# Attention projections as three fp32r products of high and low parts, and an earlier transpose of x

## The chip, the cores and the metric

The kernel is one program on one NeuronCore of a Trainium2 chip. Its engines run side by side, each with its own instruction queue: TensorE (PE; its weight loads are listed as PEld), VectorE (DVE), ScalarE (ACT), GpSimd (POOL) and SyncE (SP). They wait for each other through semaphores. The metric is the device time of one launch in microseconds, lower is better.

## The reference, cut to what matters

Three blocks follow each other on 8192 tokens of width 256, in fp32: an expert block, a linear attention, and the expert block again.

```python
x = x + 0.5 * _L0_ffn_ref(_layernorm(x), Wr, W1, W3, W2)   # 8 experts, top 2, capacity 2560
x = x + _L0_attn_ref(_layernorm(x), Wq, Wk, Wv, Wc, Ltri)
x = x + 0.5 * _L0_ffn_ref(_layernorm(x), Wr, W1, W3, W2)

def _L0_attn_ref(X, Wq, Wk, Wv, Wc, Ltri):                 # 4 sequences of 2048, 16 heads of 16
    Q, K, V = ((X @ W.T).reshape(B, L, H, d) for W in (Wq, Wk, Wv))
    KVc = cumsum(einsum('blhd,blhe->blhde', K, V), axis=1) # causal, no softmax
    Y = einsum('blhd,blhde->blhe', Q, KVc)
    Bm = tril(Ltri) @ swapaxes(tril(Ltri))
    Y = einsum('hed,blhd->blhe', Bm, Y).reshape(B, L, D)
    return Y @ Wc.T
```

## The kernel before

Four phases run one after the other. `route_phase` normalizes x, takes the router's logits and writes a table of tokens by expert; it also centres the attention's weights (`Setup`). `expert_phase` runs twice. Between its two runs, `middle_phase` does the attention, the second norm and the second routing. The expert phases already multiply through `mm3` (lines 79 to 83): each fp32 operand is kept as a high part rounded to fp32r and a low part, the rest, and a product is high x high + high x low + low x high, three fp32r matmuls.

The change is in `middle_phase`. It treats 64 chunks of 128 tokens, in 8 groups of 8. The order is written out by hand: the loop over `STEPS` is unrolled, and step n does on every engine, in program order, work of several chunks. c is the chunk's place in its group. On PE a step is: the products for q and k of chunk n+2 (`project_qk`, 8 fp32 matmuls of 128x128 weights on 128 columns), from c = 3 on the ranks of the router, v and the logits of n+2 (`project_v`, 2 matmuls of 264 columns), the scores of n+1 (`scores`, 8 matmuls on 32-row tiles), the state's product of n (`attend_state`) and the masked scores by v (`attend`, 16 matmuls on 32-column tiles), the state's update (`update`), two transposes of k (`turn_k`), two transposes of x of n+3 (`turn_x`), and the output product of n (`project_out`). One fp32 matmul shows in the trace as two records of PE and two of PEld.

ACT copies results out of PSUM: k, v, logits, q three times, then y (`keep_y`), k's rows (`keep_krow`) and the transposed x (`keep_x`), which `project_qk` of the next step waits for. DVE masks the scores of n+1 (`mask`, four operations), masks the state (`keep_state`), adds the attention's output to x (`add_out`, which the next `attend` waits for, `x2_ready`) and takes statistics. In the steps with c = 0, 1, 3 and 4, from the second group on, DVE also does the group's norms and routing, and at the end of `place_rest` (c = 3) POOL starts 16 indirect DMAs which write the table, 128 rows of 8 bytes each. `turn_x` writes into the PSUM bank `xv`, which also holds v, the logits and the ranks; so it waits until v was kept (`v_kept`) and, for c = 3, until the ranks were read (`rank_read`).

Of the kernel before, what the change touches and what calls it, by code (L numbers as in the profile page):

```python
# [382 lines left out]
class Setup:  # L383


    def __init__(self, m, k, inputs, bank_b, bank_m):
        self.k, self.inputs, self.pb, self.pm = k, inputs, bank_b, bank_m
        self.raw_qk = m.sb("su_raw_qk", [P, KD, 2 * D])
        self.raw_vr = m.sb("su_raw_vr", [P, KD, WV])
        self.wc_ext = m.sb("su_wc_ext", [P, KD, WV])  # L390
        self.wcn = m.sb("su_wcn", [P, KD, D])
        self.lt = m.sb("su_lt", [P, KD, HD])
        self.low = m.sb("su_low", [P, P])
        self.mean = m.sb("su_mean", [P, P])
# [5 lines left out]
        self.tri_ready = m.sem("su_tri_ready")  # L400
        self.bbd_made, self.bbd_ready = m.sem("su_bbd_made"), m.sem("su_bbd_ready")
        self.wcr_made, self.wcr_ready = m.sem("su_wcr_made"), m.sem("su_wcr_ready")
        self.fold_made = m.sem("su_fold_made")
# [84 lines left out]
        ins.then_inc(self.means_made, 1)  # L488

    def center(self, dve):  # L490

        k = self.k
        dve.wait_ge(self.means_made, 1)
        for kk in range(KD):
            dve.tensor_tensor(k.wqk[:, kk, :], self.raw_qk[:, kk, :], self.pm[:, 0:2 * D], ALU.subtract)
            ins = dve.tensor_tensor(k.wvr[:, kk, :], self.raw_vr[:, kk, :], self.pb[:, 0:WV], ALU.subtract)
        ins.then_inc(self.centered, 1)

    def heads(self, pe):

        pe.wait_ge(self.tri_ready, KD)
        pe.wait_ge(self.centered, 1)
        for a in range(KD):
            ins = pe.matmul(self.pb[:, a * P:(a + 1) * P], self.lbd[:, a, :], self.lbd[:, a, :], start=True, stop=True)
        ins.then_inc(self.bbd_made, 1)
        for a in range(KD):
            for kk in range(KD):
                ins = pe.matmul(self.pm[:, a * E:(a + 1) * E], self.wcn[:, kk, a * P:(a + 1) * P],
                                self.k.wvr[:, kk, D:WV], start=(kk == 0), stop=(kk == KD - 1))
        ins.then_inc(self.wcr_made, 1)  # L510

    def keep_heads(self, act):
# [52 lines left out]
def route_phase(nc, k, attention, x_in, xn_out, x1_out, out, tables, w, slot_a, raw, raw_loaded, tiles_out):  # L565
# [4 lines left out]
    with ExitStack() as ctx:  # L570
# [30 lines left out]
        with nc.Block() as block:  # L601
# [25 lines left out]
            def _(act):  # L627
# [8 lines left out]
                def step(g, s, i):  # L636
                    act.wait_ge(x_loaded[s], 16 * i + 16)
                    act.dma_start(group(x1_g, g), xin[s][:]).then_inc(x_copied[s], 16)
                    r.keep_xnT(act, g)
                    act.dma_start(group(xn_g, g), xn[s][:]).then_inc(xn_stored[s], 16)  # L640
                    r.weigh(act, g)
                    if isinstance(g, int) and g == 1:
                        su.keep_heads(act)

                rounds(act, step)
                su.keep_fold(act)
# [8 lines left out]
            def _(dve):  # L655
# [5 lines left out]
                def step(g, s, i, last=False):  # L661
                    r.choose(dve, g)
                    r.place(dve, g, s, 16 * NR * TOPK * i)
                    if not last:
                        ln(g + 2, s, i + 1)
                    if isinstance(g, int) and g == 0:
                        su.center(dve)

                su.numbers(dve)
                dve.memset(zeros[:], 0.0)  # L670
# [322 lines left out]
def middle_phase(nc, k, x1_in, xn_out, x2_out, table, tiles_out):  # L993
# [6 lines left out]
    with ExitStack() as ctx:  # L1000
# [4 lines left out]
        xT = [m.sb(f"xT{b}", [P, KD, P]) for b in range(2)]  # L1005
# [18 lines left out]
        n1_ready = m.sem("n1_ready")  # L1024
        n2_ready = m.sem("n2_ready")
        xt_made = m.sem("xt_made")
        xT_ready = m.sem("xT_ready")
        qk_made = m.sem("qk_made")
        k_kept = m.sem("k_kept")
# [29 lines left out]
        with nc.Block() as block:  # L1059
# [28 lines left out]
            def _(pe):  # L1088
# [9 lines left out]
                def project_qk(n):  # L1098
                    pe.wait_ge(xT_ready, n + 1)
                    wait(pe, kr_kept, n)  # L1100
                    for blk in range(2 * KD):
                        for kk in range(KD):
                            ins = pe.matmul(qk[:, blk * P:(blk + 1) * P], k.wqk[:, kk, blk * P:(blk + 1) * P],
                                            xT[n % 2][:, kk, :], start=(kk == 0), stop=(kk == KD - 1))
                    ins.then_inc(qk_made, 1)

                def project_v(n):
                    for kk in range(KD):
                        ins = pe.matmul(xv[:, 0:WV], xT[n % 2][:, kk, :], k.wvr[:, kk, :],
                                        start=(kk == 0), stop=(kk == KD - 1))  # L1110
                    ins.then_inc(v_made, 1)

                def scores(n):
# [57 lines left out]
                for n in STEPS:  # L1171
# [6 lines left out]
                        project_v(n + 2)  # L1178
                    if chunk(n + 1):
                        scores(n + 1)  # L1180
                    if chunk(n):
                        attend(n)
                        update(n)
                    if chunk(n + 2):
                        turn_k(n + 2)
                    if chunk(n + 3):
                        if c == 3 and g >= 1:
                            pe.wait_ge(r.rank_read, g)
                        turn_x(n + 3)
                    if chunk(n):  # L1190
                        project_out(n)
                r.count(pe, MGS)
# [2 lines left out]
            def _(act):  # L1195
                def keep_x(n):
                    act.wait_ge(xt_made, n + 1)
                    act.activation(xT[n % 2][:], xv[:, 0:D].rearrange("p (a t) -> p a t", a=KD),
                                   ACT.Copy).then_inc(xT_ready, 1)

                def keep_k(n):
                    act.wait_ge(qk_made, n + 1)
# [38 lines left out]
                for n in STEPS:  # L1241
# [3 lines left out]
                    if chunk(n + 2):  # L1245
                        keep_k(n + 2)
                        keep_v(n + 2)
                        keep_q(n + 2)
                    if chunk(n):
# [3 lines left out]
                    if chunk(n + 3):  # L1253
                        keep_x(n + 3)
# [5 lines left out]
            def _(dve):  # L1260
# [8 lines left out]
                def keep_state(n):  # L1269
                    if n % CB == CB - 1:  # L1270
# [35 lines left out]
                for c in range(MG):  # L1306
                    stats_x1(0, c)
                moments_x1(0)
                for n in STEPS:
                    g, c = divmod(n, MG)  # L1310
                    if c == 3 and g >= 1:
# [1 line left out]
                        r.place_first(dve, g - 1)  # L1313
                    if chunk(n + 1):
                        mask(n + 1)
                    if chunk(n):
                        keep_state(n)
                    if c == 0 and g >= 1:
# [16 lines left out]
class Constants:  # L1335


    def __init__(self, m):
# [17 lines left out]
        self.wqk = m.sb("wqk", [P, KD, 2 * D])  # L1356
        self.wvr = m.sb("wvr", [P, KD, WV])
        self.fold = m.sb("fold", [P, KD, WV])


# [45 lines left out]
```

## Time and profile before

| what | value |
|---|---|
| time, median of 3 runs | 3372.84 us (3371.47 to 3377.68) |
| the profiled execution's own time | 3342.54 us |
| its span, first to last instruction | 3340.8 us |
| mean granted TensorE clock | 0.940 of full speed |
| PE / PEld busy | 2977.2 / 2868.5 us, 89% / 86% |
| DVE, ACT, POOL busy | 1416.7, 1200.6, 1175.6 us |

Busy times of engines overlap. A PE record's duration is that of one matmul from start to modelled end, and consecutive ones overlap, so the pace of a run of matmuls is read from its starts: (length of the merged row less one record's duration) / (count less one). A granted clock of 1.00 is 2.4 GHz, 0.50 is 1.2 GHz. The profiled execution was 30 us shorter than the median of the timed runs.

### The profile page before, as it was taken

Reading aid. Unit: us, or ns where it says so; the run is one execution under the profiler, and the core shown is the slowest. Engines: PE = TensorE matmul, PEld = TensorE weight load, DVE = VectorE, ACT = ScalarE, POOL = GpSimd, SP = SyncE. Lnnn points to the kernel's source line nnn. Section 1 sums busy time; section 2 is a strip of 40 time slices with the busy share of each in tenths; the row PEclk is TensorE's granted clock in tenths of the full one; section 3 lists DMA queues with packets and bytes.
Section 4 is the critical chain, followed back from the end, with each engine's and each line's share of the span. In section 5 each row is a group of like instructions: output and inputs, shape, how many; then the busy total and the mean of one; then the engine's idle time right before and its main releaser. Section 6 shows DMA issues by size and latency. Waiting matters only on the chain. (4 is left out here: it accounts for less than half of the span.)

```text
span 3340.8 us, 68238 instructions
## 1 busy us (share of the span) xinstructions
PE 2977.2 (89%) x25886; PEld 2868.5 (86%) x25887; DVE 1416.7 (42%) x3386; ACT 1200.6 (36%) x2383; POOL 1175.6 (35%) x1520
## 2 busy tenths in 40 slices
PE   3429999999999999979877888499999999999998
PEld 3319999999999999968766666499999999999998
DVE  5533343443434434326655555334343434434342
ACT  1113343443434434324333333234343434434343
POOL 4563333343333333320222211433333333333333
PEclk7559999999999999989988889699999999999999
DMA  6423131222213121120111101321331322223111
GB/s 206 128 78 68 31 70 28 67 49 49 65 31 69 28 66 31 30 55 27 39 39 39 52 27 33 95 50 28 69 66 28 69 31 64 55 44 66 28 31 28
DMA packets 153036, 180.48 MB, mean 54 GB/s; under 512 B 22064, under 2 KB 126768, under 8 KB 152944
## 3 DMA queue, kind: packets, MB, share of 16 engines
q0 software_dynamic: 61376, 72.67, 13.7%
q1 hardware_dynamic: 73824, 88.72, 8.6%
q10 hardware_dynamic: 17744, 17.89, 1.6%
q8 instruction: 55, 0.90, 0.1%
q14 instruction: 37, 0.30, 0.0%
HBM read 107.84 MB, written 71.37 MB: 54 GB/s over the span
## 5 line engine op out<-in xcount | busy, mean ns | idle before, releaser
L975 DVE TENSOR_TENSOR e_hid<-e_ps,e_gate 128x512 f32<-128x512 f32 x540 | 373.2, 691 | 1048.6 <-ACT e_gate L935 1012.1
L81 PE MATMUL e_ps<-e_xT_hi,c_wa_hi 128*128 128x256 f32 x2144 | 608.0, 284 | 3.9 <-DVE e_xT_lo L969 3.0
L81 PE MATMUL e_ps<-e_xT_hi,e_wb_hi 128*128 128x256 f32 x2176 | 609.5, 280 | 0.0
L82 PE MATMUL e_ps<-e_xT_lo,e_wb_hi 128*128 128x256 f32 x2176 | 609.1, 280 | 0.0
L83 PE MATMUL e_ps<-e_xT_hi,e_wb_lo 128*128 128x256 f32 x2176 | 609.0, 280 | 0.0
L82 PE MATMUL e_ps<-e_xT_lo,c_wa_hi 128*128 128x256 f32 x2144 | 607.5, 283 | 0.0
L83 PE MATMUL e_ps<-e_xT_hi,c_wa_lo 128*128 128x256 f32 x2144 | 603.5, 281 | 0.0
L979 DVE TENSOR_TENSOR e_h_lo<-e_hid,e_h_hi 128x512 fp32r<-128x512 f32 x540 | 374.3, 693 | 376.9 <-ACT e_h_hi L937 295.3
L935 ACT ACTIVATE e_gate<-e_ps 128x512 f32<-128x512 f32 x540 | 322.0, 596 | 545.1 <-PE e_ps L83 519.6
L937 ACT ACTIVATE e_h_hi<-e_hid 128x512 fp32r<-128x512 f32 x540 | 341.3, 632 | 421.6 <-DVE e_hid L975 407.5
L813 POOL DMA_INDIRECT x<-e_yrow,e_y_token x140 | 225.5, 1611 | 655.4 <-ACT e_yrow L948 632.4
L813 POOL DMA_INDIRECT out<-e_yrow,e_y_token x138 | 222.4, 1611 | 652.8 <-ACT e_yrow L948 350.4
L82 PEld LDWEIGHTS e_ps<-e_xT_lo,e_wb_hi 128*128 128x128 f32 x2176 | 409.4, 188 | 0.0
L83 PEld LDWEIGHTS e_ps<-e_xT_hi,e_wb_lo 128*128 128x128 f32 x2176 | 409.3, 188 | 0.0
L81 PEld LDWEIGHTS e_ps<-e_xT_hi,e_wb_hi 128*128 128x128 f32 x2176 | 409.3, 188 | 0.0
L81 PEld LDWEIGHTS e_ps<-e_xT_hi,c_wa_hi 128*128 128x128 f32 x2144 | 404.1, 188 | 5.9 <-issue 5.9
L83 PEld LDWEIGHTS e_ps<-e_xT_hi,c_wa_lo 128*128 128x128 f32 x2144 | 408.3, 190 | 0.0
L82 PEld LDWEIGHTS e_ps<-e_xT_lo,c_wa_hi 128*128 128x128 f32 x2144 | 404.2, 189 | 0.0
L805 POOL DMA_INDIRECT e_xrow<-normed_rows,e_token x274 | 332.4, 1213 | 176.9 <-POOL e_token L834 118.7
L81 PE MATMUL e_psy<-e_wb_hi,e_h_hi 128*128 128x256 f32 x1088 | 313.2, 288 | 0.0
L353 POOL DMA_INDIRECT table<-mi_r_entry,mi_r_entry_at x128 | 125.3, 979 | 517.5 <-DVE mi_r_entry_at L347 364.2
L83 PE MATMUL e_psy<-e_wb_hi,e_h_lo 128*128 128x256 f32 x1088 | 307.2, 282 | 0.0
(232 smaller groups left out, 5447.1 us busy)
## 6 DMA issues: line engine op xcount, KB each, us to landing
raw<-w SPq DMA_DIRECT2D x204, 256.0 KB
r_xin<-x SPq DMA_DIRECT2D x8, 1024.0 KB
x<-r_xin ACTq DMA_DIRECT2D x8, 1024.0 KB
normed_rows<-r_xn ACTq DMA_DIRECT2D x8, 1024.0 KB
mi_x<-x SPq DMA_DIRECT2D x8, 1024.0 KB, 8.0
out<-mi_x SPq DMA_DIRECT2D x8, 1024.0 KB, 5.3
normed_rows<-mi_xn SPq DMA_DIRECT2D x8, 1024.0 KB
e_xrow<-normed_rows,e_token POOLq DMA_INDIRECT x274
```

What stands on the lines that cost most here:

```text
L81: pe.matmul(out, a[0], b[0], start=first, stop=False)
L82: pe.matmul(out, a[0], b[1], start=False, stop=False)
L83: return pe.matmul(out, a[1], b[0], start=False, stop=last)
L353: pool.indirect_dma_start(self.table, bass.IndirectOffsetOnAxis(ap=self.entry_at[b][:, c, j:j + 1], axis=0), self.entry[b][:, c, j, :], No ...
L805: pool.indirect_dma_start(xrow[:, sub, :], None, xn, bass.IndirectOffsetOnAxis(ap=token[:, sub:sub + 1], axis=0), bounds_check=ROWS - 1, o ...
L813: pool.indirect_dma_start(acc, bass.IndirectOffsetOnAxis(ap=y_token[:, sub:sub + 1], axis=0), yrow[:, sub, :], None, bounds_check=ROWS - 1 ...
L935: act.activation(gate[:, j % 2, :], ps1[j % 2][:], ACT.Silu).then_inc(gated, 1)
L937: act.activation(h[0][:, j * 512:(j + 1) * 512], hid[:, j % 2, :], ACT.Copy).then_inc(h_high, 1)
L975: dve.tensor_tensor(hid[:, j % 2, :], ps3[j % 2][:], gate[:, j % 2, :], ALU.mult).then_inc(hid_ready, 1)
L979: dve.tensor_tensor(h[1][:, at], hid[:, j % 2, :], h[0][:, at].bitcast(F32), ALU.subtract).then_inc(h_ready, 1)
```

## The change

The weights of q, k, v and logits are kept in high and low parts, split once in `Setup` (two operations on ACT, two on DVE; the heads' product reads the unsplit ones). `xT` has a high part, which ACT's `keep_x` now writes rounded to fp32r, and a low part, which a new DVE operation `low_x` writes (PSUM less high part). The products go through `mm3`. On PE `turn_x` of n+3 stands in front of `attend`, on ACT `keep_x` in front of `keep_y`, on DVE `low_x` between `mask` and `keep_state`.

```diff
     def center(self, dve):
         for kk in range(KD):
-            dve.tensor_tensor(k.wqk[:, kk, :], self.raw_qk[:, kk, :], self.pm[:, 0:2 * D], ALU.subtract)
-            ins = dve.tensor_tensor(k.wvr[:, kk, :], self.raw_vr[:, kk, :], self.pb[:, 0:WV], ALU.subtract)
+            dve.tensor_tensor(self.raw_qk[:, kk, :], self.raw_qk[:, kk, :], self.pm[:, 0:2 * D], ALU.subtract)
+            ins = dve.tensor_tensor(self.raw_vr[:, kk, :], self.raw_vr[:, kk, :], self.pb[:, 0:WV], ALU.subtract)
+    def split_high(self, act):
+        act.wait_ge(self.centered, 1)
+        act.activation(self.k.wqk[0][:], self.raw_qk[:], ACT.Copy)
+        act.activation(self.k.wvr[0][:], self.raw_vr[:], ACT.Copy).then_inc(self.w_split, 1)
+    def split_low(self, dve):
+        dve.wait_ge(self.w_split, 1)
+        dve.tensor_tensor(k.wqk[1][:], self.raw_qk[:], k.wqk[0][:].bitcast(F32), ALU.subtract)
+        dve.tensor_tensor(k.wvr[1][:], self.raw_vr[:], k.wvr[0][:].bitcast(F32), ALU.subtract)
...
                 def project_qk(n):
-                            ins = pe.matmul(qk[:, blk * P:(blk + 1) * P], k.wqk[:, kk, blk * P:(blk + 1) * P],
-                                            xT[n % 2][:, kk, :], start=(kk == 0), stop=(kk == KD - 1))
+                            ins = mm3(pe, qk[:, blk * P:(blk + 1) * P],
+                                      [w[:, kk, blk * P:(blk + 1) * P] for w in k.wqk],
+                                      [t[:, kk, :] for t in xT[n % 2]], kk == 0, kk == KD - 1)
                 def project_v(n):
-                        ins = pe.matmul(xv[:, 0:WV], xT[n % 2][:, kk, :], k.wvr[:, kk, :],
-                                        start=(kk == 0), stop=(kk == KD - 1))
+                        ins = mm3(pe, xv[:, 0:WV], [t[:, kk, :] for t in xT[n % 2]], [w[:, kk, :] for w in k.wvr],
+                                  kk == 0, kk == KD - 1)
...
                     if chunk(n + 1):
                         scores(n + 1)
+                    if chunk(n + 3):
+                        if c == 3 and g >= 1:
+                            pe.wait_ge(r.rank_read, g)
+                        turn_x(n + 3)
                     if chunk(n):
                         attend(n)
                         update(n)
                     if chunk(n + 2):
                         turn_k(n + 2)
-                    if chunk(n + 3):
-                        if c == 3 and g >= 1:
-                            pe.wait_ge(r.rank_read, g)
-                        turn_x(n + 3)
...
+                def low_x(n):
+                    dve.wait_ge(xT_high, n + 1)
+                    dve.tensor_tensor(xT[n % 2][1][:], xv[:, 0:D].rearrange("p (a t) -> p a t", a=KD),
+                                      xT[n % 2][0][:].bitcast(F32), ALU.subtract).then_inc(xT_ready, 1)
...
                     if chunk(n + 1):
                         mask(n + 1)
+                    if chunk(n + 3):
+                        low_x(n + 3)
                     if chunk(n):
                         keep_state(n)
```

One ordinary step on PE, before: `mi_qk` and `mi_xv` are the PSUM banks of q/k and of v/x, `c_wqk` and `c_wvr` the weights, `mi_sc` the scores, `mi_yo` the attention's output, `mi_kv` the state.

```order
755 L1103 MATMUL mi_qk<-mi_xT0,c_wqk 128x128 x8
756 L1109 MATMUL mi_xv<-c_wvr,mi_xT0 128x264 x2
757 L1119 MATMUL mi_sc<-mi_qeo1,mi_kT1 128x256 x8
758 L1127 MATMUL mi_yo<-mi_qT1,mi_state0 128x128 x2
759 L1139 MATMUL mi_yo<-mi_prob0,mi_vpad1 32x128 x16
760 L1153 MATMUL mi_kv<-mi_vpad1,mi_krow0 128x128 x2
761 L1160 MATMUL mi_qk<-c_ident,mi_kT0 128x128 x2
762 L1094 MATMUL mi_xv<-c_ident,mi_x1 128x128 x2
763 L1166 MATMUL mi_yo<-c_fold,mi_yT0 128x264 x2
```

The same step of the changed kernel, from the last of its 24 matmuls for q and k:

```order
946 L83 MATMUL mi_qk<-mi_xT_hi0,c_wqk_lo 128x128
947 L81 MATMUL mi_xv<-c_wvr_hi,mi_xT_hi0 128x264
948 L82 MATMUL mi_xv<-c_wvr_lo,mi_xT_hi0 128x264
949 L83 MATMUL mi_xv<-c_wvr_hi,mi_xT_lo0 128x264
950 L81 MATMUL mi_xv<-c_wvr_hi,mi_xT_hi0 128x264
951 L82 MATMUL mi_xv<-c_wvr_lo,mi_xT_hi0 128x264
952 L83 MATMUL mi_xv<-c_wvr_hi,mi_xT_lo0 128x264
953 L1134 MATMUL mi_sc<-mi_qeo1,mi_kT1 128x256 x8
954 L1108 MATMUL mi_xv<-c_ident,mi_x1 128x128 x2
955 L1142 MATMUL mi_yo<-mi_qT1,mi_state0 128x128 x2
956 L1154 MATMUL mi_yo<-mi_prob0,mi_vpad1 32x128 x16
```

The transposes of x moved from behind those of k to behind the scores, and the two projections are 24 and 6 matmuls instead of 8 and 2.

On DVE, a step with c = 1 of the changed kernel (`mi_prob` is the masked scores, `mi_state` the masked state, `mi_r_lg` the router's logits):

```order
508 L1307 SCALAR_TENSOR_TENSOR mi_x2<-mi_yo,mi_n11_rstd,mi_x1 128x256
509 L133 BN_STATS mi_n21_stats<-mi_x2 128x6
509 L133 BN_STATS mi_n10_stats<-mi_x1 128x6 x2
510 L1280 TENSOR_TENSOR mi_prob0<-mi_sc,c_causal 128x512 x4
511 L1295 TENSOR_TENSOR mi_xT_lo0<-mi_xv,mi_xT_hi0 128x256
512 L1289 TENSOR_TENSOR mi_state0<-mi_kv,c_same_head 128x256
513 L264 TENSOR_TENSOR mi_r_lg<-mi_lgs,mi_n20_rstd 128x64
```

Line 511 is new; all the rest stands as before, one place later.

## Rows read from the trace of the kernel before

**Rows 1.** The attention phase as one window, columns as in rows 2.
```profile
1483.00:2097.00 614.00, 507.58 (x5415) 415.04 (x5415) 350.12 (x1282) 224.29 (x649) 109.61 (x112) 0.90 0.12 39
```

**Rows 2.** Windows of steps 23, 25 to 29: us, PE, PEld, DVE, ACT, POOL, clock.
```profile
1703.98:1711.35 7.37, 7.37 (x85) 6.16 (x84) 3.86 (x8) 2.97 (x9) 0.00 (x0) 1.00 0.00 0
...
1718.73:1726.59 7.86, 7.44 (x85) 6.16 (x84) 6.49 (x26) 3.22 (x10) 0.00 (x0) 1.00 0.15 50
1726.59:1734.34 7.75, 7.45 (x86) 6.16 (x85) 7.27 (x41) 4.15 (x13) 0.00 (x0) 1.00 0.00 0
1734.34:1742.02 7.68, 7.68 (x94) 6.46 (x93) 5.53 (x17) 3.93 (x12) 0.00 (x0) 1.00 0.01 2
1742.02:1763.08 21.06, 9.23 (x85) 6.67 (x83) 6.03 (x22) 3.74 (x12) 14.20 (x15) 0.77 0.02 2
1763.08:1772.38 9.30, 9.30 (x85) 8.08 (x85) 3.71 (x23) 3.89 (x11) 1.46 (x2) 0.79 0.35 116
```

**Rows 3.** Timeline of step 23: start us, us, engine, line, instruction, idle before it.
```profile
1703.98 1.95 PE L1103 MATMUL mi_qk<-mi_xT,c_wqk 128*128 128x128 f32 x16
1705.76 1.06 PE L1109 MATMUL mi_xv<-c_wvr,mi_xT 128*128 128x264 f32 x4
1706.75 1.15 PE L1119 MATMUL mi_sc<-mi_qeo,mi_kT 32*128 32x256 f32 x16
...
1707.22 0.17 ACT L1220 ACTIVATE mi_lgx<-mi_xv 128x8 f32<-128x8 f32 x1
...
1707.82 0.71 PE L1127 MATMUL mi_yo<-mi_qT,mi_state 128*128 128x128 f32 x4
1707.96 2.48 DVE L1265 TENSOR_TENSOR mi_prob<-mi_sc,c_causal 128x512 f32<-128x512 f32 x4 [2.70 <-PE mi_sc L1119]
...
1710.36 0.42 DVE L1274 TENSOR_TENSOR mi_state<-mi_kv,c_same_head 128x256 f32<-128x256 f32 x1
```

**Rows 4.** Pace of matmuls: timeline, instructions by line, one window in the experts.
```profile
35.43 3.64 PE L249 MATMUL r_lg<-c_wr,r_r_xnT 128*128 128x8 f32 x32
...
L249 PEld LDWEIGHTS r_lg<-c_wr,r_r_xnT x256: 186/333/338, 17.2 to 197.2; 128*128 128x128 f32 x128
...
L81 PEld LDWEIGHTS e_ps<-e_xT_hi,e_wb_hi x2176: 186/188/194, 419.4 to 3322.1; 128*128 128x128 f32 x198
...
L302 PEld LDWEIGHTS mi_xv<-mi_r_chosen,c_ones x56: 95/96/131, 1583.3 to 2093.9; 128*128 128x128 bf16 x56
...
1300.00:1310.00 10.00, 10.00 (x86) 1.00 0.06 2
```

**Rows 5.** Timeline of DVE in steps 24 to 27.
```profile
1718.24 0.64 DVE L138 BATCH_NORM_AGGREGATE mi_n_mv<-mi_n_stats 128x2 f32<-128x6 f32 x8
...
1724.04 2.47 DVE L1265 TENSOR_TENSOR mi_prob<-mi_sc,c_causal 128x512 f32<-128x512 f32 x4
1726.42 0.41 DVE L1274 TENSOR_TENSOR mi_state<-mi_kv,c_same_head 128x256 f32<-128x256 f32 x1
...
1731.78 2.47 DVE L1265 TENSOR_TENSOR mi_prob<-mi_sc,c_causal 128x512 f32<-128x512 f32 x4
...
1738.10 0.22 DVE L315 TENSOR_TENSOR mi_r_pos<-mi_xv,c_region 128x64 f32<-128x64 f32 x1 [1.83 <-ACT mi_lgx L1220]
...
1739.63 2.48 DVE L1265 TENSOR_TENSOR mi_prob<-mi_sc,c_causal 128x512 f32<-128x512 f32 x4
```

**Rows 6.** Timeline of step 28, from POOL's first indirect DMA.
```profile
1744.62 0.98 POOL L353 DMA_INDIRECT table<-mi_r_entry,mi_r_entry_at  x1 [58.05 <-DVE mi_r_entry_at L347]
...
1758.13 0.38 ACT L1224 ACTIVATE mi_yT<-mi_yo 128x256 f32<-128x256 f32 x1 [11.69 <-remote]
...
1763.08 3.78 PE L1103 MATMUL mi_qk<-mi_xT,c_wqk 128*128 128x128 f32 x16 [2.39 <-ACT mi_xT L1198]
...
1767.32 0.23 DVE L1285 SCALAR_TENSOR_TENSOR mi_lgs<-mi_yo,mi_n_rstd,mi_lgx 128x8 f32<-128x8 f32 x1 [6.63 <-remote]
```

**Rows 7.** Timeline of the route phase, DVE behind POOL's second batch.
```profile
83.94 0.22 DVE L257 TENSOR_SCALAR r_r_lg<-r_lg 128x64 f32<-128x64 f32 x1 [13.79 <-remote]
```

More of the change, by code:

```diff
@@ L400, in __init__ @@
         self.tri_ready = m.sem("su_tri_ready")
+        self.w_split = m.sem("su_w_split")
         self.bbd_made, self.bbd_ready = m.sem("su_bbd_made"), m.sem("su_bbd_ready")
@@ L490, in center @@
     def center(self, dve):
-        k = self.k
         dve.wait_ge(self.means_made, 1)
         for kk in range(KD):
-            dve.tensor_tensor(k.wqk[:, kk, :], self.raw_qk[:, kk, :], self.pm[:, 0:2 * D], ALU.subtract)
-            ins = dve.tensor_tensor(k.wvr[:, kk, :], self.raw_vr[:, kk, :], self.pb[:, 0:WV], ALU.subtract)
+            dve.tensor_tensor(self.raw_qk[:, kk, :], self.raw_qk[:, kk, :], self.pm[:, 0:2 * D], ALU.subtract)
+            ins = dve.tensor_tensor(self.raw_vr[:, kk, :], self.raw_vr[:, kk, :], self.pb[:, 0:WV], ALU.subtract)
         ins.then_inc(self.centered, 1)
+    def split_high(self, act):
[3 more added lines that the diff above has]
+    def split_low(self, dve):
+        k = self.k
+        dve.wait_ge(self.w_split, 1)
+        dve.tensor_tensor(k.wqk[1][:], self.raw_qk[:], k.wqk[0][:].bitcast(F32), ALU.subtract)
+        dve.tensor_tensor(k.wvr[1][:], self.raw_vr[:], k.wvr[0][:].bitcast(F32), ALU.subtract)
     def heads(self, pe):
@@ L508, in heads @@
                 ins = pe.matmul(self.pm[:, a * E:(a + 1) * E], self.wcn[:, kk, a * P:(a + 1) * P],
-                                self.k.wvr[:, kk, D:WV], start=(kk == 0), stop=(kk == KD - 1))
+                                self.raw_vr[:, kk, D:WV], start=(kk == 0), stop=(kk == KD - 1))
         ins.then_inc(self.wcr_made, 1)
@@ L643, in step @@
                         su.keep_heads(act)
+                        su.split_high(act)
                 rounds(act, step)
@@ L667, in step @@
                         su.center(dve)
+                    if isinstance(g, int) and g == 1:
+                        su.split_low(dve)
                 su.numbers(dve)
@@ L1004, in middle_phase @@
         xn2 = m.sb("xn2", [P, 2, MG, D])
-        xT = [m.sb(f"xT{b}", [P, KD, P]) for b in range(2)]
+        xT = [[m.sb(f"xT_{part}{b}", [P, KD, P], F32R) for part in ("hi", "lo")] for b in range(2)]
         qT = [m.sb(f"qT{b}", [P, KD, P]) for b in range(3)]
@@ L1026, in middle_phase @@
         xt_made = m.sem("xt_made")
+        xT_high = m.sem("xT_high")
         xT_ready = m.sem("xT_ready")
@@ L1197, in keep_x @@
                     act.wait_ge(xt_made, n + 1)
-                    act.activation(xT[n % 2][:], xv[:, 0:D].rearrange("p (a t) -> p a t", a=KD),
-                                   ACT.Copy).then_inc(xT_ready, 1)
+                    act.activation(xT[n % 2][0][:], xv[:, 0:D].rearrange("p (a t) -> p a t", a=KD),
+                                   ACT.Copy).then_inc(xT_high, 1)
                 def keep_k(n):
@@ L1248, in _ @@
                         keep_q(n + 2)
+                    if chunk(n + 3):
+                        keep_x(n + 3)
                     if chunk(n):
@@ L1252, in _ @@
                         keep_krow(n + 2)
-                    if chunk(n + 3):
-                        keep_x(n + 3)
                     if 1 <= c <= 4 and g >= 1:
@@ L1308, in _ @@
                 moments_x1(0)
+                low_x(0)
                 for n in STEPS:
@@ L1315, in _ @@
                         mask(n + 1)
+                    if chunk(n + 3):
+                        low_x(n + 3)
                     if chunk(n):
@@ L1355, in __init__ @@
         self.wr = m.sb("wr", [P, KD, E])
-        self.wqk = m.sb("wqk", [P, KD, 2 * D])
-        self.wvr = m.sb("wvr", [P, KD, WV])
+        self.wqk = [m.sb("wqk_hi", [P, KD, 2 * D], F32R), m.sb("wqk_lo", [P, KD, 2 * D], F32R)]
+        self.wvr = [m.sb("wvr_hi", [P, KD, WV], F32R), m.sb("wvr_lo", [P, KD, WV], F32R)]
         self.fold = m.sb("fold", [P, KD, WV])
```

## The prediction, made before the changed kernel ran

> **What bounds the kernel now.** I read the split by phases first, then the attention phase step by step, then one step's timeline. (Each of rows 1 and 2 gives busy time in the order PE, PEld, DVE, ACT, POOL.) The changed projections run only between 1483 and 2097 us, 614 us in all, in which PE is busy 507.6, DVE 350.1 and ACT 224.3 us [rows 1]. The reader is to see in the windows that an ordinary step takes 7.37 us and PE has work in all of it, while DVE has 3.86 and ACT 2.97 us [rows 2]: there PE is the bound, and what the change adds to PE goes into the time one for one. The steps with c = 1, 2 and 3 are different: they take 7.86, 7.75 and 7.68 us, and DVE is busy 6.49, 7.27 and 5.53 of them [rows 2]; DVE is nearly as much the bound as PE. The step with c = 4 takes 21.06 us, of which PE has work in 9.23. It is no ordinary wait: from 3 us after POOL's first indirect DMA, ACT waits 11.69 us for the result of `attend`, and the groups behind it come through one by one, the output product's only at 1767.3 [rows 6]. PE's results come at a crawl as long as POOL issues its 16 table writes.
>
> **The q and k projection.** It removes 16 passes (8 fp32 matmuls, two records each) and adds 24 fp32r matmuls of 128 columns. The 16 took 1705.76 - 1703.98 = 1.78 us, 0.111 each [rows 3]. No row shows an fp32r matmul of 128 columns, so its pace is bounded. From above by the same type on twice the columns: 86 matmuls, nearly all fp32r of 256 columns, in 10 us, 0.116 each [rows 4]. From below by the stream alone: 256 fp32r columns in 0.116 makes 0.058 for 128. What decides is the weight load. L249 streams 8 columns only, and its 32 passes still come (3.64 - 0.18)/31 = 0.112 us apart at full clock (the 0.18 is one record) [rows 4]. So a 128x128 fp32 weight load alone holds the array 0.11 us, whatever streams behind it. Is an fp32r load the same? Its shortest record is 186 ns, as L249's, against 95 for a bf16 load [rows 4]: same load, same floor. I take 0.116, between ends 0.112 and 0.125 (some slack for the change of operand order) if the floor holds. 24 x 0.116 = 2.78, less 1.78: +1.00 us a step.
>
> The Trainium skill, "TensorE: Matmul & The Clock Gate", section "Back-to-back issue gap", gives about 81 ns as the sustained pace of a weight load and a matmul at 128 columns. By it the 24 would take 1.94 us, +0.16. The trace does not bear that out for fp32: 112 ns with 8 columns. I keep it as a rival. The same page, Part 3, says that weight loads overlap matmuls in flight only if the row group differs. By that load and stream would add up; but 256 columns at 0.116 with a load that alone needs 0.112 leave no room for a sum, so the trace speaks against that one, too.
>
> **The v and logits projection.** Four passes of 264 columns and the change to 32-row tiles took 1706.75 - 1705.76 = 0.99 us [rows 3], about 0.225 a pass and 0.09. Now six fp32r matmuls of 264 columns, 0.116 to 0.12 each: 0.79. That is -0.19. Sum of both: **+0.81 us** per ordinary step, 8.18 instead of 7.37 (with 0.112: +0.7; with 0.125: +1.0).
>
> **The moved transposes.** They cost PE the same two records in either place. At their new place they wait for ACT to have kept v and the logits, which was done at 1707.39, 0.43 us before the product behind the scores began [rows 3], so nothing. ACT writes the high part as soon as q is kept, before y is ready. The output product follows two transposes sooner behind `attend` than before; that can cost at most these two records, 0.2 us, if y should come late. In the step shown PE waits for nobody, so I take 0.
>
> **The low part on DVE.** One subtraction 128x256 from PSUM; nearest row the state's mask, 0.41 to 0.42 us [rows 3]. In an ordinary step it stands behind the mask of the scores: scores now start at 3.57 in the step, the mask 1.21 later at 4.8 (1707.96 less 1706.75) [rows 3], 2.4 us, low part ready at 7.7. The next projection is due at 8.18: hidden with 0.5 us to spare. That cover is gone in the tight steps, all times from the start of the step's q and k products:
> - c = 0: 8.18 (+0.81). DVE's norms start behind the state, at 8.1.
> - c = 1: from the norm's start to the next mask DVE needs 1724.04 - 1718.24 = 5.8 us [rows 5], so this mask starts at 8.1 + 5.8 - 8.18 = 5.7, and 2.4 and 0.41 later the low part is ready: 8.55 instead of 7.86, +0.7.
> - c = 2: from the state's start to the next mask 1731.78 - 1726.42 = 5.36 [rows 5]; mask at 5.36, low part at 8.2: 8.2 instead of 7.75, +0.45. The waits of `attend` for `add_out`, which lengthened these two steps, are gone: PE comes there 1 us later.
> - c = 3: the mask stands behind `place_first`, which waits for the kept logits at 3.76 and starts the mask at 5.29 (1738.10 and 1739.63 [rows 5], less 1734.34 [rows 2]). Both shift by the 0.81 of PE; mask 6.1, low part at 8.95: 8.95 instead of 7.68, +1.27. PE waits here for DVE some 0.75 us.
> Sum of the four: +3.2 us.
>
> **c = 4 and 5.** PE gets its +0.81 twice. The crawl has the length of POOL's batch, about 20 us, from wherever it starts; I take what it costs as unchanged. What PE does behind it runs at half clock: 16 passes in 3.78 us [rows 6], 0.21 apart, twice the 0.111. 24 of them are +1.7 us instead of +1.0, and v gains 0.38 instead of 0.19: +0.5 more. Sum +2.1. Of the four results that come late one by one before the next projection can start, the x transposes are no longer one; at up to 2 us each that could give back 0 to 2 us a group. I take 0 since PE works the same list off during the crawl.
>
> **c = 6 and 7:** 2 x 0.81 = +1.6.
>
> **Sum.** A group with routing: 3.2 + 2.1 + 1.6 = 6.9, seven of them 48.5. The first group has none: 8 x 0.81 = 6.5. The two projections at the start at half clock: +1. In the route phase the split of the weights puts some 2.5 us on ACT and 2.5 on DVE (1552 columns per partition each at the 0.41 us per 256), where DVE then idles 13.79 us behind POOL's batch [rows 7]: hidden, 0.5 for the rest. The experts are untouched. Total **+57 us**. On the profiled execution's 3342.5 us (span 3340.8 and 1.7 around it) that makes 3399.5. The timed runs lie 30 us above the profiled one; I put the difference on their median: 3372.8 + 57 = **3430 us**, +1.7%.
>
> **The rivals.**
> - A, fp32r at 128 columns runs no faster than the fp32 product it stands for, two passes or 0.223 each (256 columns is the only width the trace shows). Then +3.57 - 0.19 = +3.4 a step, 64 steps: +216, 3590. For it: no row at 128. Against it: the pace per column is the type's, and 264 of v isn't concerned. 6%.
> - B, load and stream do not overlap: 0.112 + 0.053 = 0.165, +1.98 a step, about +127, 3500. 4%.
> - C, faster: an fp32r load is quick as bf16's (95 ns records against 186) and the stream decides, 0.058. Then -0.39 - 0.19 = -0.58 a step where PE binds. It decides from 0.082 down: there PE's sum is zero. DVE's new 0.41 then binds c = 1 to 3 and costs +1 there; a group 1 - 5 x 0.58 = -1.9, the whole -13 - 5 = -18: 3355. Against it the length of the load records. 6%.
> - D, 0.081 to 0.085 as in the skill's pace: PE's sum is zero, and DVE's low part costs about 1 us a group: +7, 3380, at the edge of no change. 4%.
> - E, within my forecast: the crawl gets shorter by 2 us a group (-14), or longer, because more of `attend` falls into it (+14).
>
> **How the numbers follow.** About 0.2% (7 us) is what a measurement can tell from no change. Forecast with E: 80%. Its own range: 0.112 takes 0.1 off the steps where PE binds, 6 in all, and with the shorter crawl 51 - 14 = +37; 0.125 adds 0.22 to each of 64, and with the longer crawl 71 + 14 = +85. The outer ends need two things at once; I give 3405 to 3458, which leaves out A to D. Faster: C, 6%. Same: half of D and a little, 3%. Slower: 91%.
>
> **What would show it.** In the changed profile the 24 matmuls of L81 to L83 into `mi_qk` start 0.112 to 0.118 us apart at full clock, with load records of about 188 ns; ordinary steps take 8.1 to 8.3 us with PE busy throughout; in c = 3 PE waits for DVE's low part; the windows outside 1483 to 2150 stay as they are. It is wrong if the pace is below 0.09 or above 0.13, if ordinary steps show PE waiting for `xT_lo`, or if the step with c = 4 changes by more than 3 us.

## The result, and the profile after

| what | before | after |
|---|---|---|
| time, median of 4 runs each, on one chip | 3372.15 us (3365.35 to 3377.68) | 3460.09 us (3456.95 to 3460.75) |
| ratio after / before | | 1.026, 95% interval 1.024 to 1.028 |
| profiled execution, span | 3340.8 us | 3458.8 us |
| mean granted TensorE clock | 0.940 | 0.926 |

The changed kernel is 88 us slower. The forecast was slower by 57, 3430 us in a range up to 3458: the direction was right, 31 us were missing.

The same steps as in [rows 2], as windows of the changed kernel: the attention phase, then steps 23 to 29 (us, then PE, PEld, DVE, ACT, POOL busy, clock, DMA).

```profile
1478.90:2170.00 691.10, 559.21 (x5851) 478.59 (x5851) 355.35 (x1258) 216.44 (x626) 104.46 (x109) 0.86 0.11 34
1759.62:1767.69 8.07, 8.07 (x97) 7.12 (x95) 4.20 (x9) 2.98 (x9) 0.00 (x0) 1.00 0.00 0
1767.69:1775.75 8.06, 8.06 (x96) 7.11 (x95) 4.19 (x9) 2.98 (x9) 0.00 (x0) 1.00 0.78 239
1775.75:1784.10 8.35, 8.35 (x96) 7.09 (x94) 7.28 (x32) 3.40 (x11) 0.00 (x0) 1.00 0.08 26
1784.10:1792.18 8.08, 8.08 (x95) 7.05 (x95) 7.60 (x42) 3.94 (x13) 0.00 (x0) 1.00 0.01 2
1792.18:1801.15 8.97, 8.61 (x105) 7.32 (x103) 6.09 (x19) 4.58 (x13) 0.00 (x0) 1.00 0.00 0
1801.15:1827.95 26.80, 9.97 (x94) 8.23 (x95) 6.31 (x22) 4.04 (x12) 15.65 (x16) 0.73 0.02 2
1827.95:1840.42 12.47, 12.47 (x97) 10.89 (x95) 7.03 (x30) 3.24 (x10) 0.00 (x0) 0.62 0.25 85
```

The reader is to see that an ordinary step is full of PE and 0.70 us longer than before (8.07 against 7.37), that the steps with c = 1, 2 and 3 take 8.35, 8.08 and 8.97 us (forecast 8.55, 8.2 and 8.95), and that the surprise stands in the last two rows: c = 4 and 5 grew from 21.06 + 9.30 = 30.36 to 39.27 us, by 8.9, where 2.1 was forecast. Not all of the 8.9 is the change: the two profiles are of executions 118 us apart (spans 3340.8 and 3458.8), while the timed medians are 88 apart, and a second profile of the kernel before has longer steps here than the first (below).

One ordinary step in the timeline, against [rows 3]:

```profile
1759.84 0.28 PE L82 MATMUL mi_qk<-mi_xT_lo,c_wqk_hi 128*128 128x128 f32 x1
1762.30 0.27 PE L83 MATMUL mi_qk<-mi_xT_hi,c_wqk_lo 128*128 128x128 f32 x1
1762.41 0.34 PE L81 MATMUL mi_xv<-c_wvr_hi,mi_xT_hi 128*128 128x264 f32 x1
1763.29 1.15 PE L1134 MATMUL mi_sc<-mi_qeo,mi_kT 32*128 32x256 f32 x16
1764.37 0.44 PE L1108 MATMUL mi_xv<-c_ident,mi_x 128*128 128x128 f32 x2
1764.84 0.38 ACT L1213 ACTIVATE mi_xT_hi<-mi_xv 128x256 fp32r<-128x256 f32 x1
1766.90 0.41 DVE L1295 TENSOR_TENSOR mi_xT_lo<-mi_xv,mi_xT_hi 128x256 fp32r<-128x256 f32 x1
1767.69 0.39 PE L81 MATMUL mi_qk<-mi_xT_hi,c_wqk_hi 128*128 128x128 f32 x1
```

From the step's start (1759.62) to the first matmul for v (1762.41) the 24 matmuls take 2.79 us, 0.116 each; that includes a longer gap behind the first. From the second (1759.84) to the last (1762.30) they come 0.112 apart. v with the change to the scores takes 1763.29 - 1762.41 = 0.88. Both together are 3.67 us, where before they were 2.77 (1.78 + 0.99); the rest of the step gave 0.2 back. The low part is ready at 1767.31, 7.69 in the step and 0.38 before PE wants it.

The step with c = 4, against [rows 6]:

```profile
1803.87 0.98 POOL L353 DMA_INDIRECT table<-mi_r_entry,mi_r_entry_at  x1 [69.53 <-DVE mi_r_entry_at L347]
1806.66 1.19 PE L1154 MATMUL mi_yo<-mi_prob,mi_vpad 128*32 128x128 f32 x30
1807.42 0.38 ACT L1213 ACTIVATE mi_xT_hi<-mi_xv 128x256 fp32r<-128x256 f32 x1 [1.00 <-PE mi_xv L1108]
1823.11 0.98 POOL L353 DMA_INDIRECT table<-mi_r_entry,mi_r_entry_at  x1 [0.30 <-issue]
1825.96 0.38 ACT L1239 ACTIVATE mi_yT<-mi_yo 128x256 f32<-128x256 f32 x1 [18.16 <-remote]
1826.71 0.42 DVE L1289 TENSOR_TENSOR mi_state<-mi_kv,c_same_head 128x256 f32<-128x256 f32 x1 [17.20 <-remote]
```

PE now reaches `attend` later behind the start of the batch: it begins 1806.66 - 1803.87 = 2.79 us behind POOL's first write (2.65 to 3.06 over the groups), where it began at most 1.9 behind it before. ACT then waits 18.16 us for y, not 11.69, and gets it 22.1 us behind the first write (18.7 to 22.9 over the groups), 13.5 before (10.7 to 13.5). And the start of the phase, which had no row in the forecast:

```profile
1492.33 2.71 DVE L133 BATCH_NORM_STATS2 mi_n_stats<-mi_x 128x6 f32<-128x256 f32 x8 [5.11 <-DMA mi_x<-x]
1493.14 0.38 ACT L1213 ACTIVATE mi_xT_hi<-mi_xv 128x256 fp32r<-128x256 f32 x1 [17.66 <-PE mi_xv L1108]
1498.86 0.42 DVE L1295 TENSOR_TENSOR mi_xT_lo<-mi_xv,mi_xT_hi 128x256 fp32r<-128x256 f32 x1
1499.33 0.47 PE L81 MATMUL mi_qk<-mi_xT_hi,c_wqk_hi 128*128 128x128 f32 x1 [6.29 <-DVE mi_xT_lo L1295]
```

The first projection now waits 6.29 us for a low part that stands behind all of DVE's statistics of the first group; before, it needed only ACT's copy, which was there after 0.53 us:

```profile
1483.29 3.78 PE L1103 MATMUL mi_qk<-mi_xT,c_wqk 128*128 128x128 f32 x16 [0.53 <-ACT mi_xT L1198]
```

The clock follows: from the first transposes of x to the first scores the changed kernel takes 23.4 us, all of them at a granted clock of 0.50, the kernel before 15.3 us at 0.61, and 1.00 from there on, where the changed kernel still has 0.50 up to 1528.

### The profile page after: what moved, and what is told of

Same layout as the page of the kernel before. It is cut to its first block and busy times, and to the rows that moved or that the text cites. A ratio compares the mean times of both kernels' runs of the same rounds, so it can differ in the third digit from the quotient of the medians.

```text
span 3458.8 us, 69586 instructions
## 1 busy us (share of the span) xinstructions
PE 3037.9 (88%) x26526; PEld 2939.3 (85%) x26527; DVE 1441.7 (42%) x3452; ACT 1204.6 (35%) x2385; POOL 1175.9 (34%) x1520
## 3 DMA queue, kind: packets, MB, share of 16 engines
q0 software_dynamic: 61376, 72.67, 12.8%
```

## The experiments

Theory 1 was that the price in ordinary steps is as forecast, and that what is missing is PE's results behind POOL's batch: PE takes some 0.6 us per pass there, whatever the size of the pass, and the change leaves more passes of `attend` inside. Against it stood rivals, above all that the moved transposes cost the time, and that where the batch falls in the step does not matter. The expectations number them. They count the step with c = 4 from its scores to the next step's scores (20.8 to 25.5 us in the first profile, 29.3 to 30.7 in the changed kernel's), and so do the lengths of these steps given below; the windows above count from its q and k products. Each group of runs was on one chip with the kernel before beside it; differences between kernels are compared within a group, or as ratios.

**The first chip: before 3372.52 us (3366.15 to 3381.91, 7 runs).**

*e1, the transposes back at their old place, the low part behind the state.* The edit on PE; ACT's copy and DVE's low part move in the same way.

```diff
-                    if chunk(n + 3):
...
-                        turn_x(n + 3)
                     if chunk(n):
                         attend(n)
                         update(n)
                     if chunk(n + 2):
                         turn_k(n + 2)
+                    if chunk(n + 3):
...
+                        turn_x(n + 3)
```

> The changed kernel with the transposes of x, ACT's high part and DVE's low part (now behind the state's mask) back at their old places; only the arithmetic is changed. Theory 1 (during POOL's 16 table writes PE gets through one matmul pass in some 0.65 us, whatever its size, and the 32 passes of attend now fall into that stretch because POOL's first write comes 3.06 us before attend, not 1.89): here POOL starts still about 3.1 us before attend, so the step with c = 4 stays at 29 to 31 us and the time within 10 us of 3460. Rival 2 (the moved transposes push attend into the slow stretch): attend comes 0.22 us earlier, y is released 2 to 4 us earlier in each of seven groups: 3430 to 3445.

Measured: 3480.48 us (3478.46 to 3481.13), ratio 1.0314 (1.0289 to 1.0339), against 1.026 of the changed kernel. The ordinary step is 8.48 us, 0.41 over the changed kernel's:

```profile
1772.65 0.38 PE L1108 MATMUL mi_xv<-c_ident,mi_x 128*128 128x128 f32 x2
1773.54 0.42 DVE L1295 TENSOR_TENSOR mi_xT_lo<-mi_xv,mi_xT_hi 128x256 fp32r<-128x256 f32 x1 [0.36 <-ACT mi_xT_hi L1213]
1774.02 0.33 PE L81 MATMUL mi_qk<-mi_xT_hi,c_wqk_hi 128*128 128x128 f32 x1
```

The low part ends at 1773.96 and PE starts right behind it. So the move costs nothing; it keeps a chain of transpose, ACT, DVE off the step's end, and `attend` is as late behind the batch without it (2.8 to 3.2 us), with steps c = 4 of 29.6 to 30.4 us, as expected. The rival that the move costs time falls. That the time would stay within 10 us of 3460, as theory 1 had it, missed: it is 20 away, since the part of the low part was not in it.

*e3, the first low part ahead of the statistics.*

```diff
                 r.start(dve)
+                low_x(0)
                 for c in range(MG):
                     stats_x1(0, c)
                 moments_x1(0)
-                low_x(0)
```

> The changed kernel with DVE's very first low part put in front of the first group's statistics. In the trace of the changed kernel the first projection waits 6.3 us for it. Theory: the attention phase starts 5 to 6 us earlier, time 3454. Rival (the half-clock stretch at the start sets it, the wait is hidden in it): no change, 3460.

Measured: 3450.36 us (3449.45 to 3458.02), ratio 1.0233 (1.0205 to 1.026); from the first transposes of x to the first scores 18.09 us instead of 23.38. The wait at the start is real and avoidable, worth 5 us in the profile; by the time alone it is not clear of the changed kernel, whose ratio (1.024 to 1.028) touches this one:

```profile
1492.23 0.42 DVE L1295 TENSOR_TENSOR mi_xT_lo<-mi_xv,mi_xT_hi 128x256 fp32r<-128x256 f32 x1 [6.32 <-ACT mi_xT_hi L1213]
1492.58 2.70 DVE L133 BATCH_NORM_STATS2 mi_n_stats<-mi_x 128x6 f32<-128x256 f32 x8
```

*e4 and e5, the kernels before and after without the attention phase's 128 indirect writes* (the second expert phase then works on unfilled entries).

```diff
-                for g in range(MGS):
-                    r.enter(pool, g, g % 2)
...
```

> The kernel before without the 128 indirect DMAs of the attention phase that write the second routing table (the second expert phase then works on unfilled entries, with the same counts). Theory 1: the long steps with c = 4 (21 to 25 us) become ordinary ones of 7.4 to 8, and the half-clock stretches go: seven groups lose 15 to 17 us each, 3372 - 112 = 3260. Rival (these steps wait for something else, as code loading or the router's chain): within 10 us of 3372.

> The changed kernel without the same 128 indirect DMAs. Theory 1: no step over 9 us; seven groups lose some 22 us each, 3460 - 154 = 3306; and against the kernel before without writes it is +50 to +65 us (0.69 us a step, the tight steps, the start) instead of +88. Rival 3 (the extra of the step with c = 4 comes from the low part's hand-over, ACT to DVE to PE): the difference between the two kernels without writes stays 80 to 90 us.

Measured: 3213.51 us (3211.41 to 3214.97), ratio 0.9523, and 3272.04 us (3265.51 to 3274.03), ratio 0.9692. Their distance is **58.5 us**, against 88 with the writes: the change without the writes costs what was forecast (50 to 65 were expected), and some 29 us come with them. Both times are below theory 1's, which had 3260 and 3306, in part because the last batch, which the second experts wait for, is gone too: from the last output product to their first matmul e4 takes 27.4 us, the kernel before 51.1. In the kernel before without writes the step with c = 4 is an ordinary one:

```profile
1725.41:1732.79 7.38, 7.38 (x85) 6.16 (x85) 5.40 (x20) 3.95 (x11) 0.00 (x0) 1.00 0.15 53
```

**The second chip: before 3340.15 us (3333.47 to 3344.42, 7 runs).** The first run here is the kernel before again.

> The kernel before, profiled once more. Its first profile lies 30 us under its timed runs. If that profile was a quick execution, this one shows a time near 3370 us, a route phase some 10 us longer (the first expert matmul at 267 to 272 us instead of 258, as in every other profile so far), and in the attention phase results of attend released later than 13.5 us behind POOL's first write. If profiling itself makes it quicker, it shows 3342 again.

Its profiled execution took 3349.39 us, with steps c = 4 of 21.1 to 26.6 us and y 11.4 to 13.6 us behind the first write. Neither expectation is decided, since this chip's own timed runs are at 3340; but a profiled execution is not quicker than timed ones here. So the profile that the forecast rested on was most likely taken on a quicker chip than its timed runs; the chip of the first profile is not on record.

*e6, the changed kernel, each batch held back until the scores of the step with c = 4; e7 and e8, after and before with two writes behind the scores of each of eight steps.*

```diff
                 for g in range(MGS):
+                    wait_alone(pool, sc_made, min(8 * g + 14, NCH), k.passed)
                     r.enter(pool, g, g % 2)
```

```diff
                 for g in range(MGS):
-                    r.enter(pool, g, g % 2)
+                    wait_alone(pool, r.entry_ready, g + 1, k.passed)
+                    for c in range(MG):
+                        if c % 1 == 0:
+                            wait_alone(pool, sc_made, min(8 * g + 14 + c // 1, NCH), k.passed)
+                        for j in range(TOPK):
+                            pool.indirect_dma_start(
...
```

> The changed kernel, but POOL starts each batch of 16 table writes only when the scores of the c = 4 step are made, some 3.4 us later. Theory 1 (a pass costs about 0.65 us in the slow stretch, whatever its size): the stretch now falls on the next step's projections, 30 long passes worth 3.4 us of ordinary time, instead of attend's 32 short ones worth 1.0; steps c = 4 and 5 together 34.5 instead of 39.2 us, time 3428. Rival 4 (the stretch costs its own length wherever it falls): 3460.

> The changed kernel with each group's 16 table writes spread over eight steps, two behind each step's scores. If the slow stretch needs a long run of writes (it sets in 2.6 us behind the first): no step over 9 us, 3272 (without writes) + 24 for the last batch behind the attention = 3296. If every write slows PE for its own 1.3 us: the same total as now, 3440 to 3460.

> The kernel before with its table writes spread in the same way. Slow stretch gone: 3213.5 + 24 = 3238. If every write has its own share of it: 3360 to 3375.

Measured: e6 3414.42 us (3410.93 to 3417.97), ratio 1.0227 (1.0209 to 1.0246); e7 3386.72 (3380.17 to 3391.16), 1.0135 (1.0112 to 1.0158); e8 3314.9 (3311.18 to 3318.19), **0.9925 (0.9906 to 0.9944)**. Holding the batch back takes all 32 passes of `attend` out of it, and c = 4 and 5 together come down from 39.4 to 35.0 us (means of groups 1 to 6), close to the 34.5 of theory 1. The time is not: 3428 us on the first chip would be a ratio of 1.0165. The measured one, compared across two chips, moves in that direction, but it lies nearer to the rival's 1.026, and its interval touches the changed kernel's, which was not timed on this chip. So theory 1 has the place right and the size only in part. Spreading neither removes the cost nor keeps it whole: both expectations of e7 (ratios of 0.977, or 1.020 to 1.026) and of e8 (0.960, or 0.996 to 1.001) miss. In e7 nearly every step with two writes takes 9.8 us, 1.7 more than 8.07 (10.1 with c = 3, and 13.0 with c = 0 in the last three groups):

```profile
1732.06 0.98 POOL L1102 DMA_INDIRECT table<-mi_r_entry,mi_r_entry_at  x1 [7.56 <-PE mi_sc L1142]
1733.34 0.98 POOL L1102 DMA_INDIRECT table<-mi_r_entry,mi_r_entry_at  x1 [0.30 <-issue]
1734.90 0.38 ACT L1247 ACTIVATE mi_yT<-mi_yo 128x256 f32<-128x256 f32 x1 [2.94 <-remote]
```

8 x 1.7 = 13.6 us a group, against 23 for the batch in the changed kernel (39.4 for c = 4 and 5, 16.15 in e5). Here `attend` begins 0.14 us ahead of the first write, and y, due 1.15 us behind that start as in an undisturbed step, comes 2.84 us behind the write. So the lateness does not need a long run of writes and does not set in only at 2.6 us, as the expectation of e7 had it. e8 is the one version with all of the writes that beat the kernel before, by 0.75%, on this chip.

**The third chip: before 3189.2 us (3187.09 to 3192.51, 13 runs).**

> The kernel before, unchanged, for a profile on the same chip as the three kernels of this group. If chips differ in the length of the stretch behind the 16 table writes, its steps c = 4 lie elsewhere than 21.1 to 26.6 us (the two profiles so far); if not, they lie there again, and the sum of groups 1 to 7 is 522 to 532 us.

> The changed kernel, unchanged, beside the kernel before and two kernels with late writes on one chip. Theory 1 (the change loses about 29 us behind the writes, wherever it runs): ratio 1.024 to 1.028 again, step c = 4 at 29 to 31 us. Rival (part of the 88 us belonged to the chip of that comparison): ratio 1.020 or less.

> The changed kernel with each batch of 16 writes held back until the scores of its step c = 4 are done, so that attend's 32 passes lie ahead of the slow stretch. Theory 1 (PE does its passes there at about 0.65 us each for a fixed time of some 20 us, so what counts is how cheap the passes are that fall into it; 32 passes of attend at 0.03 us replaced by dearer ones give back 32 x (0.12 - 0.03) = 2.9 us a group): 15 to 22 us less than the changed kernel in the same comparison. Rival (the place of the batch in the step does not matter): within 5 us of it.

> The kernel before with the same hold. Theory 1: 16 of attend's passes (4 in some groups) leave the slow stretch, 16 x (0.11 - 0.03) = 1.3 us a group, 9 us less than the kernel before (ratio 0.9965 to 0.9985), and the distance to the changed kernel with the hold comes down to 60 to 70 us, from 88. Rival (the place does not matter): within 3 us of the kernel before, and the distance stays above 75 us.

Measured: the profiled execution of before 3189.14 us; after **3251.91** (3250.99 to 3253.93), ratio **1.0196 (1.0179 to 1.0213)**; e6 again 3254.27 (3253.52 to 3254.85), 1.0204; e9 (the same hold in the kernel before) 3189.24 (3186.7 to 3190.93), 0.9999. On this chip nothing is late behind the batch: y comes 2.6 to 3.0 us behind the first write, 3.8 to 4.2 in the changed kernel. The kernel before, in the same step as [rows 6]:

```profile
1672.54 0.98 POOL L353 DMA_INDIRECT table<-mi_r_entry,mi_r_entry_at  x1 [39.95 <-DVE mi_r_entry_at L347]
1674.43 1.08 PE L1139 MATMUL mi_yo<-mi_prob,mi_vpad 128*32 128x128 f32 x32
1675.58 0.38 ACT L1224 ACTIVATE mi_yT<-mi_yo 128x256 f32<-128x256 f32 x1 [1.21 <-PE mi_yo L1139]
1691.80 0.98 POOL L353 DMA_INDIRECT table<-mi_r_entry,mi_r_entry_at  x1 [0.30 <-issue]
```

Its windows of steps 26 to 29, and those of steps 27 and 28 of the changed kernel:

```profile
1654.51:1662.25 7.74, 7.45 (x85) 6.16 (x84) 7.26 (x41) 4.15 (x13) 0.00 (x0) 1.00 0.00 0
1662.25:1669.94 7.69, 7.69 (x94) 6.46 (x93) 5.53 (x17) 3.94 (x12) 0.00 (x0) 1.00 0.01 2
1669.94:1677.32 7.38, 7.38 (x86) 6.16 (x84) 5.94 (x22) 3.94 (x12) 3.87 (x4) 1.00 0.02 3
1677.32:1684.69 7.37, 7.37 (x85) 6.16 (x84) 5.75 (x28) 3.69 (x11) 5.54 (x7) 1.00 0.45 144
```

```profile
1697.66:1706.63 8.97, 8.61 (x105) 7.31 (x103) 6.09 (x19) 4.58 (x13) 0.00 (x0) 1.00 0.01 2
1706.63:1714.64 8.01, 8.01 (x94) 7.07 (x95) 6.22 (x22) 3.27 (x11) 4.07 (x5) 1.00 0.01 1
```

It is the same program in the same order: `attend` starts 1.89 us behind the first write as it did in [rows 6], POOL issues its 16 writes over the same 20.2 us, and the steps with c = 2 and 3 are the same to 0.01 us. Yet y is kept 3.04 us behind the first write and not 13.5, and c = 4 takes 7.38 us and not 21.06. So the late results belong to the chip (or to the state it was in), together with the batch. Here the change costs 3251.91 - 3189.2 = **62.7 us**; the rival that part of the 88 belongs to the chip holds, and theory 1 in the form that 29 us are lost wherever the kernel runs is refuted. e6 again and e9 show that the hold itself costs nothing much, and on this chip can tell nothing more: their distance of 65.0 us lies in theory 1's 60 to 70, but so does the 62.7 without the hold.

**The fourth chip: before 3344.58 us (3338.18 to 3352.32, 15 runs); the late results are there.** Which part of the batch makes them late? Theories are numbered anew. In the kernel before, the 128 writes were replaced; the second expert phase works on unfilled entries in all three. What stands in place of `enter`, in e10 (rows of 512 bytes), e11 (plain DMAs) and e12 (reads):

```diff
+                            pool.indirect_dma_start(
+                                wide, bass.IndirectOffsetOnAxis(ap=r.entry_at[g % 2][:, c, j:j + 1], axis=0),
+                                wide_row[:], None,
...
+                            pool.dma_start(plain[g, c, j], r.entry[g % 2][:, c, j, :]).then_inc(r.entered[g % 2], 16)
...
+                            pool.indirect_dma_start(
+                                got[:, g, c, j, :], None, table,
+                                bass.IndirectOffsetOnAxis(ap=r.entry_at[g % 2][:, c, j:j + 1], axis=0),
```

> The kernel before with the attention phase's 128 indirect writes of 128 rows of 8 bytes replaced by as many indirect writes of 128 rows of 512 bytes, by the same indices, into another tensor (the second experts then work on unfilled entries). Only a chip on which the kernel before shows the slow stretch says anything: there the kernel before takes over 3300 us and leaving the writes out gave a ratio of 0.952. Theory 1 (PE's results come late because the engines that carry out indirect writes of tiny rows are held): ratio 0.95 to 0.965, steps c = 4 at 7.4 to 9 us. Theory 2 (it is POOL's issuing of any indirect DMA, whatever its rows): ratio 0.99 to 1.01, steps c = 4 at 21 to 27 us.

> The same 8-byte entries, written by 128 plain DMAs from POOL's queue to consecutive rows of another tensor (no indices). Theory 1 (tiny rows): steps c = 4 at 21 to 27 us as before, ratio 0.99 to 1.01. Theory 2 (the indirect form, with its indices): 7.4 to 9 us, ratio 0.95 to 0.965.

> As many indirect DMAs with the same indices in the other direction, 128 rows of 8 bytes read from the table into SBUF (the second experts again work on unfilled entries). If it is the indirect form on POOL (theory 2) or tiny rows in any direction (theory 1): c = 4 at 21 to 27 us, ratio 0.99 to 1.01. If it is writing to DRAM in tiny rows only: 7.4 to 9 us, ratio 0.95 to 0.965.

Measured: e10 3341.35 us (3337.7 to 3350.1), ratio 0.9992 (0.9983 to 1.0002), steps c = 4 of 22.9 to 26.4 us; e11 3214.68 (3213.12 to 3217.99), 0.9611 (0.9594 to 0.9629), steps of 7.38; e12 3332.65 (3328.87 to 3335.87), 0.9964 (0.995 to 0.9977), steps of 17.1 to 23.3. In e10 y is about as late as in [rows 6], 12.8 us behind the first write (1744.40), where it was 13.5:

```profile
1757.20 0.38 ACT L1235 ACTIVATE mi_yT<-mi_yo 128x256 f32<-128x256 f32 x1 [10.97 <-remote]
```

and in e11 a batch is

```profile
1647.05 8.48 POOL L1087 DMA_DIRECT2D plain<-mi_r_entry  x16 [50.59 <-DVE mi_r_entry_at L347]
```

Theory 2 holds as far as this goes: it comes with the indirect form on POOL, whatever the size of the rows and in either direction. Neither tiny rows nor writing to DRAM is needed. Two things differ in e11 beside the form: a plain batch is over in 8.5 us, an indirect one in 20.2, and its rows lie one behind the other, where the indices of the others scatter them. Whether it is the form, the scattered rows or POOL's longer work is not separated; within the 8.5 us nothing is late, y coming 3.3 us behind the first DMA with `attend` at 2.2.

## Why the prediction was wrong in size and right in direction

**The pace of fp32r at 128 columns: right.** Shown by the timeline: 0.112 us apart, the bound from the load, and 0.116 with the gap behind the first, which is what was taken. The load records are as long as forecast:

```profile
L81 PEld LDWEIGHTS mi_qk<-mi_xT_hi,c_wqk_hi x512: 186/192/337, 1499.3 to 2187.3; 128*128 128x128 f32 x171
```

Rivals A (0.223), B (0.165), C (0.058) and D (0.081) fall with it; the pace that the Trainium skill, "TensorE: Matmul & The Clock Gate", section "Back-to-back issue gap", gives for 128 columns (81 ns) does not hold for this type here.

**The sum of an ordinary step: +0.70 instead of +0.81.** For q and k it was +1.01, as said; v gained 0.11 and not 0.19. Together +0.90, but 0.2 came back behind them. The sum is 0.11 a step too high, 5 to 6 us over the phase.

**The moved transposes at 0: right, and the low part hidden: right,** ready at 7.69 in the step, where 7.7 was forecast. What I had not worked out is that the move was needed: without it (e1) the low part stands on the path, 0.41 us a step.

**c = 1, 2, 3: right** (8.35, 8.08, 8.97 against 8.55, 8.2, 8.95), DVE's low part being last in c = 3. PE stands idle there for 0.36 us (8.61 busy of 8.97), not for 0.75.

**The start: missed.** "The two projections at the start at half clock: +1". The low part of chunk 0 is queued on DVE behind eight statistics and the moments, which I did not look at; with it PE waits 6.29 us, and the stretch at half clock is longer: first scores 8.4 us later on the third chip, and 4.9 us more than forecast in the first group's steps, of which the first takes 10.7 us there, where it took 6.8 before.

**c = 4 and 5: this is the step that failed.** The prediction said: "The crawl has the length of POOL's batch, about 20 us, from wherever it starts; I take what it costs as unchanged." The batch's length stayed, what it costs did not: y came 22.1 us behind its first write and not 13.5, and what is behind it ran at a granted clock of 0.62, where it had 0.79. Read together, the runs say that it counts how late behind the first write a result is due; e6 alone varied this on purpose. Where the third chip has y at 0.9 us (e6), 3.0 (before) and 3.9 (after, the group of the windows), it came at 3.5, 13.5 and 22.1 on the chips with the late results. The forecast shifted PE by 0.81 us in each step, and what that does to `attend` in the crawl entered its sum as nothing; 0.9 us more in what is due cost 8.6 us of y. The prediction's own sign of being wrong, a step with c = 4 changed by more than 3 us, came true (5.7). Rival E had both directions, the longer one by this very cause ("more of `attend` falls into it"), but at no more than 14 us; it was 25 to 29. The wait in [rows 6] was also misread: its 11.69 us begin 1.8 us behind the first write (1758.13 - 11.69 - 1744.62), not 3.

The third chip allows the sum without it. Its two profiles, beside the terms of the forecast:

| stretch | forecast | third chip |
|---|---|---|
| seven groups with routing | +48.5 | +41.3 |
| first group | +6.5 | +11.4 |
| first transposes to first scores | +1 | +8.4 |
| all the rest | +0.5 | +2.5 |
| span | +57 | +63.5 (timed 62.7) |

So 88 is 57, plus about 6 for terms of the right kind and wrong size (the start and the first group too low by 12, the groups with routing too high by 7), plus 25 for the late results: 88 less 62.7. The pair without writes gives 88 - 58.5 = 29.5 for the last part. That these are 25 to 29 us rests on comparisons across groups of runs: the changed kernel was not timed again beside e4 and e5, and the 25 compares two chips. That they come with the writes is shown; why a pass takes so long there is not.

The time itself had a second weakness: 3372.8 is one chip's. The same kernel took 3189, 3340, 3345 and 3372 us on four. The first profile's span is 153 us longer than that on the third chip, and nearly all of it lies where POOL issues indirect DMAs in batches: 38 ahead of the first experts, 114 in groups 1 to 7.

## What to carry to other kernels

Where a profile shows results that come late beside another engine's batch, their cost does not move as a block with the batch: count what of the bound engine's work falls into it before and after, since it can grow when the step gets longer, as it did here. A low part adds a link (transpose, ACT, DVE) to each operand's chain; leave it room before its next use (0.38 us here; behind the state's mask it cost 0.41 us a step), and look at the first one separately, since the queue in front of it is another. Before a few per cent are put down to a change, see whether the kernel before is the same on another chip.

## What the runs showed of the hardware that was not expected

- While POOL issues indirect DMAs back to back (one per 1.28 us), PE's results come late. The later a result is due behind the first DMA, the more: y due at 0.9, 3.0 and 3.9 us came at 3.5, 13.5 and 22.1. For the 32 passes of `attend` in the changed kernel, begun at 2.8 us, that is an estimated (22.1 - 2.8) / 32 = 0.6 us per pass, where they need 1.1 us in all. Many records of PE's starts go on as planned (30 of the 32 passes within 1.2 us); what waits for PE shows it, as a release from "remote". ACT's and DVE's own operations keep their durations.
- It was there on three of the four chips with groups of runs, and on one not at all, with the same program. Two indirect DMAs in a step cost 1.7 us where it is there (e7, e8); 16 in a row 15 to 24. Rows of 8 or of 512 bytes, writes or reads: the same time within 0.4% (e10, e12). Plain DMAs of the same bytes to consecutive rows: none of it (e11).
- Why PE is held, and why on some chips alone, stays open. Nothing in the traces tells it.
